# Experts stages of a six-stage transformer kernel: the bias-and-push product on 32-row groups, layer norm sums on ScalarE's accumulator, variance on GpSimd

## The reference

```python
def _L1_ffn_ref(x, router_w, router_b, expert_w, expert_b):
    logits = jnp.einsum('bsd,ed->bse', x, router_w) + router_b
    probs = jax.nn.softmax(logits, axis=-1)
    weights = jnp.max(probs, axis=-1)
    top1 = jnp.argmax(probs, axis=-1)
    y_all = jnp.einsum('bsd,eod->bseo', x, expert_w) + expert_b
    y = jnp.take_along_axis(y_all, top1[:, :, None, None], axis=2)[:, :, 0, :]
    return y * weights[:, :, None]

x = x + 0.5 * _L1_ffn_ref(_layernorm(x), ...)
```

## Time and profile before

| | |
|---|---|
| median of 3 runs | 1595.37 us (1590.17 to 1595.67) |
| profiled execution | 1591.5 us, its span 1589.6 us |
| PE busy | 1541.5 us, 97% of the span |
| DVE busy | 1260.2 us, 79% |
| ACT busy | 936.1 us, 59% |
| POOL busy | 935.5 us, 59% |
| first E stage | about 1184 to 1251 us of the span |
| second E stage | about 1516 to 1588 us, its first batch beside attention |

### The profile page before, as it was taken

How to read it: one execution, slowest core, us unless ns; L and a number is a source line. 1 busy time by engine, 2 the same in 40 slices (tenths; PEclk the granted TensorE clock), 3 DMA queues, 4 the chain that set the end, 5 groups by cost and what they waited for, 6 DMA issues and landing times. The chain is left out here.

```text
span 1589.6 us, 43810 instructions
## 1 busy us (share of the span) xinstructions
PE 1541.5 (97%) x15808; PEld 922.1 (58%) x15808; DVE 1260.2 (79%) x2662; ACT 936.1 (59%) x1826; POOL 935.5 (59%) x806
## 2 busy tenths in 40 slices
PE   7999999999999899799999999999999999999999
PEld 4666666666666666566666666666654434444444
DVE  7976776777877788786777777768778899999877
ACT  6755555555656344365555555556553388888842
POOL 2865756757754399775766756657456334444453
PEclk9999999999999999999999999999999899999999
DMA  4300000000001242100000000000001121112011
GB/s 163 106 8 5 7 0 7 7 0 7 8 1 34 53 84 67 42 6 3 8 1 7 7 0 7 7 0 8 5 12 31 44 61 37 39 39 62 9 42 60
DMA packets 74315, 43.34 MB, mean 27 GB/s; under 512 B 53818, under 2 KB 70842, under 8 KB 74052
## 3 DMA queue, kind: packets, MB, share of 16 engines
q1 hardware_dynamic: 74180, 41.56, 10.9%
HBM read 10.47 MB, written 2.10 MB: 8 GB/s over the span
## 5 line engine op out<-in xcount | busy, mean ns | idle before, releaser
L618 POOL TENSOR_TENSOR scratch<-scratch 128x512 f16<-128x512 f32 x379 | 441.6, 1166 | 375.4 <-ACT scratch L826 375.2
L1395 DVE SCALAR_TENSOR_TENSOR scratch<-psum,scratch 128x512 f32<-128x512 f32 x512 | 352.4, 689 | 235.8 <-PE psum L1979 213.4
L821 ACT ACTIVATE scratch<-psum 128x512 f32<-128x512 f32 x512 | 305.2, 597 | 394.9 <-PE psum L1979 394.0
L2021 PE MATMUL psum<-ffn_down_hi,scratch 128*128 128x128 f16 x2048 | 369.3, 219 | 0.3
L2023 PE MATMUL psum<-ffn_down_hi,scratch 128*128 128x128 f16 x2048 | 369.2, 219 | 0.0
L2022 PE MATMUL psum<-ffn_down_lo,scratch 128*128 128x128 f16 x2048 | 369.2, 219 | 0.0
L826 ACT ACTIVATE scratch<-scratch 128x512 f16<-128x512 f32 x512 | 318.6, 622 | 12.0 <-DVE scratch L1395 11.7
L2021 PEld LDWEIGHTS psum<-ffn_down_hi,scratch 128*128 128x128 f16 x2048 | 200.3, 98 | 59.1 <-POOL scratch L618 0.7
L2022 PEld LDWEIGHTS psum<-ffn_down_lo,scratch 128*128 128x128 f16 x2048 | 200.4, 98 | 58.0
L2023 PEld LDWEIGHTS psum<-ffn_down_hi,scratch 128*128 128x128 f16 x2048 | 200.4, 98 | 0.0
L1977 PE MATMUL psum<-x_hi,ffn_gate_hi 128*128 (+1 forms) x512 | 194.5, 380 | 1.5 <-ACT scratch L821 1.5
(11 more groups left out here) (223 smaller groups left out, 2703.8 us busy)
## 6 DMA issues: line engine op xcount, KB each, us to landing
scratch<-scratch SPq DMA_DIRECT2D x96, 128.0 KB, 2.7
raw<-in_ffn_w_dram SPq DMA_DIRECT2D x8, 768.0 KB, 4.2
ffn_up_hi<-scratch SPq DMA_DIRECT2D x32, 128.0 KB, 2.8
x_tok<-in_x_dram SPq DMA_DIRECT2D x8, 256.0 KB, 7.2
out_dram<-x_tok SPq DMA_DIRECT2D x7, 256.0 KB, 2.2
raw<-in_lin_dram SPq DMA_DIRECT2D x1, 1092.0 KB
x_hi<-scratch SPq DMA_TRANSPOSE x46, 2.3
x_lo<-scratch SPq DMA_TRANSPOSE x46, 2.3
```

The source lines that it names most:

```text
L618: pool.tensor_tensor(h_lo[r], h32[r], h_hi[r], ALU.subtract).then_inc(s_plo, 1)
L821: act.activation(gate_act[k % 2], bank(k % 2), ACT.Silu, scale=W_DOWN).then_inc(s_s, 1)
L1395: dve.scalar_tensor_tensor(h32[k % HSLOTS], bank(5 + k % 2), W_DOWN, gate_act[k % 2], ALU.mult, ALU.mult).then_inc(s_h, 1)
L2021: pe.matmul(dst, h_hi[r][:, cols], hi, start=k % FC == 0 and n == 0, stop=False, skip_group_check=True)
```

## The change

1. **Bias and push on 32-row groups.** The table `e_bias` holds the ten rows (eight push, two bias) four times, at partitions 0, 32, 64 and 96, alternately for the two halves of the experts. `e_not` and `e_out` repeat the mask in each 32-row group. For two tiles at a time, behind the products of both, four matmuls of 32 rows go to four banks. In the last batch, and where the second E stage is woven into attention, it is one tile and two matmuls. The table is filled by 12 small DMAs during the second F stage.
2. **Three pairs of banks.** `expert_banks` gives most tiles one of three pairs instead of two.
3. **Router bias by one matmul.** `logits` issues one 128x32 matmul for the bias of all four tiles instead of four of 128x8.
4. **Statistics on ScalarE.** `prep_sums` (four ACTIVATEs that copy a tile with scale -1/128, the accumulator giving the negative mean `ln_neg`) and `prep_squares` (four that square x plus `ln_neg`, the accumulator giving the sum) replace VectorE's statistics in both E stages, except for batches 2 and 3 of the second. Two of them stand behind each `weigh`. GpSimd's `prep_var` makes the variance of the sums. `prep_sums` waits for the `x_norm` of the batch before, because `ln_neg` is reused.
5. **`x_upper` one tile later.** It now stands ahead of the third `weigh`, before it stood ahead of the second.
6. **No hardware loop** on PE and ACT in the E stages; the bodies are written out.

```diff
+E_GROUP = 32
 # SyncE, between turn_x(3, 0) and turn_x(3, 1)
+            for i in range(4):
+                c = slice(i % 2 * BANK, (i % 2 + 1) * BANK)
+                row = i * E_GROUP
+                sp.dma_start(e_bias[row:row + E, :], bias_w[0:E, c]).then_inc(s_ebias, 16)
+                sp.dma_start(e_bias[row + E:row + E + 1, :], bias_w[32:33, c]).then_inc(s_ebias, 16)
+                sp.dma_start(e_bias[row + E + 1:row + E + 2, :], bias_w[64:65, c]).then_inc(s_ebias, 16)
 # GpSimd
+            def prep_var(n):
+                pool.wait_ge(s_mv, n + SUB)
+                pool.tensor_scalar(ln_var[:], ln_square[:], 1.0 / C, LN_EPS, ALU.mult, ALU.add).then_inc(s_var, SUB)
                     if b + 3 < last:
+                        if not (use and b == 0):
+                            prep_var(n0 + SUB * (b + 3))
                         prep_rstd(n0 + SUB * (b + 3))
                         norm(b + 3)
 # ScalarE
+            def prep_sums(n, s, parts=range(SUB)):
+                if parts[0] == 0:
+                    act.wait_ge(s_xn, n)
+                for q in parts:
+                    ins = act.activation(ln_spent[:, q * P:(q + 1) * P], sub(x_tok, s + q), ACT.Copy, scale=-1.0 / C, accum_out=ln_neg[:, q:q + 1])
+                if parts[-1] == SUB - 1:
+                    ins.then_inc(s_bn, SUB)
+
+            def prep_squares(n, s, parts=range(SUB)):
+                if parts[0] == 0:
+                    act.wait_ge(s_bn, n + SUB)
+                    act.wait_ge(s_var, n)
+                for q in parts:
+                    ins = act.activation(ln_spent[:, q * P:(q + 1) * P], sub(x_tok, s + q), ACT.Square, bias=ln_neg[:, q:q + 1], accum_out=ln_square[:, q:q + 1])
+                if parts[-1] == SUB - 1:
+                    ins.then_inc(s_mv, SUB)
-                        if k == 1 and prep and not (isinstance(b, int) and b == 0):
+                        if k == 2 and prep and not (isinstance(b, int) and b == 0):
                             x_upper(n0 + SUB * b + LEAD)
+                        if stats:
+                            part = range(k % 2 * 2, k % 2 * 2 + 2)
+                            if k < 2:
+                                prep_sums(n0 + SUB * bx, SUB * (bx % NB), part)
+                            else:
+                                prep_squares(n0 + SUB * bx, SUB * (bx % NB), part)
 # VectorE
-                            prep_bn(n0 + SUB * (b + 3), SUB * ((b + 3) % NB))
-                        if k == 2 and b + 3 < last:
-                            statistics(b + 3)
 # TensorE
+                    router_bias = bias_w[:, E * C:E * C + E].rearrange("p (o e) -> p o e", o=1).to_broadcast([P, SUB, E])
+                    pe.matmul(by(bank(7, 0, SUB * E), SUB), ones, router_bias, start=True, stop=True)
-                    pe.wait_ge(s_epick, t + 1)
+                    pe.wait_ge(s_epick, picked_before(t))
+                    for i, k in enumerate(tiles):
+                        for half_of in range(2):
+                            rows = slice((2 * i + half_of) * E_GROUP, (2 * i + half_of + 1) * E_GROUP)
+                            ins = pe.matmul(bank(2 * expert_banks(b * SUB + k) + half_of), e_out[odd][rows, k * P:(k + 1) * P], e_bias[rows, :],
+                                            start=False, stop=True, skip_group_check=True)
+                        ins.then_inc(s_ey, 1)
-                            bias_and_others(b0 + b, k, odd)
+                            if not more:
+                                bias_and_others(b0 + b, (k,), odd)
+                            elif k % 2:
+                                bias_and_others(b0 + b, (k - 1, k), odd)
```

More of the change, by code:

```diff
@@ L650, in body @@
                         if k == 16 and f and next_weights(ph, b):
-                            for t in e_out:
-                                pool.memset(t, 1.0).then_inc(s_erows, 1)
+                            pool.memset(e_not, 1.0 / E_OUT).then_inc(s_erows, 1)
+                            pool.memset(e_bias, 0.0).then_inc(s_erows, 1)
                 body(0, False)
@@ L980, in moe @@
                     begin(act, ph["i"])
-                    others(b0, 0)
+                    others(b0, 0, 4)
                 def body(b, odd, prep, more):
+                    bx = b + 3
+                    stats = bx < (NB + 2 if ph["next"] else NB)
                     for k in range(SUB):
@@ L1660, in moe @@
                     begin(dve, ph["i"])
-                last = NB + 2 if ph["next"] else NB
                 for b in range(use, NB):
@@ L2120, in bias_and_others @@
+                def bias_and_others(b, tiles, odd):
+                    if 0 in tiles:
                         pe.wait_ge(s_eout, b + 1)
-                    for half_of in range(2):
-                        a = half_of * BANK
-                        ins = pe.matmul(bank(2 * (k % 2) + half_of), e_out[odd][:, k * P:(k + 1) * P], bias_w[:, a:a + BANK], start=False, stop=True)
-                    ins.then_inc(s_ey, 1)
-                def others(b, at=4):
+                        if b == 0:
+                            pe.wait_ge(s_ebias, 12 * 16)
+                    for i, k in enumerate(tiles):
[4 more added lines that the diff above has]
+                        ins.then_inc(s_ey, 1)
@@ L2127, in others @@
+                def others(b, at=6):
                     pe.wait_ge(s_enot, b + 1)
                     pe.wait_ge(s_eout, b)
+                    if b == NB + 2:
+                        pe.wait_ge(s_mout, NB)
                     for k in range(SUB):
-                        ins = pe.matmul(bank(at, k * P, (k + 1) * P)[0:E], e_not[:, k * E:(k + 1) * E], ident16, start=True, stop=True)
+                        ins = pe.matmul(bank(at, k * P, (k + 1) * P), e_not[:, k * P:(k + 1) * P], ident16, start=True, stop=True)
```

100 lines of the change are left out of this document (57 added, 43 removed).

## The result

The changed kernel takes 1626.15 us (median of 4 runs, 1624.36 to 1627.92) against 1593.91 (4 runs beside it, 1590.17 to 1595.67): a ratio of 1.020, 95% interval 1.019 to 1.022. It is slower by 32 us. Its profiled execution has a span of 1625.6 us where before had 1589.6, so 36.0 us are to be found between those two.

What follows compares the result with a forecast made beforehand. The late turned x was to bound the experts stages at 10.4 us a batch against 8.17. Terms of +27.2 on 1591.5 gave 1618.7, plus 3.9 of scale 1622.6, plus 3 for the clock: forecast 1625, range 1606 to 1641.

Steps and rivals of the forecast that it cites:

- The ring: Experts stages: first pick, second weigh, sums, x_upper, transfer, logits, product, bias group, next pick; 10.4 us a batch against 8.17.
- the two sums: ScalarE, between the second weigh and x_upper: two sums with accumulator delivery, 0.80 us.
- Accumulator: ScalarE's sums and squares: delivering the accumulator's result costs 0.20 us each, like a small ACTIVATE of its own.
- Bias group: TensorE: four 32-row matmuls, 0.43 us a group; 0.58 us from the products' nominal end until the pick can start.
- first stage, to the third batch: First experts stage up to the third batch's first pick: 14.3 us instead of 9.7, fourth pick 0.5 sooner; +4.1 us.
- its four middle batches: First experts stage, four middle batches at 10.4 us each instead of 8.17; +8.9 us.
- second stage, to the third batch: Second experts stage up to the third batch's first pick: 1546.7 instead of 1540.48; +6.2 us.
- its four batches: Second experts stage: three batches of 10.4 us and one without statistics of 9.6, instead of 32.63; +8.2 us.
- the clock: TensorE's clock falls to 0.50 behind two of eleven waits, up to 1.6 us each; 3 us in all.
- rival 1: TensorE's clock falls in nearly all eleven long batches: +18 us instead of +3, 1640 us; 17 in 100.
- The scale: Whole kernel: the median of the runs lies 3.9 us above the profiled execution, turning 1618.7 into 1622.6.
- a lead of 1.8 us: Before the change, steady batches: the transfer behind x_lower is done at 1208.5, the logits wanting it come at 1210.3.

Runs made afterwards that it cites:

- upper_earlier: The changed kernel with x_upper back behind the first weigh, ahead of the second; 1618.08 us, ratio 1.017.
- logits_behind_pair: The changed kernel with the next batch's logits moved behind the first pair's bias group; 1607.90 us, ratio 1.009.
- bias_singly: The changed kernel with the bias product behind each tile's own products, two 32-row matmuls at a time; 1607.05 us, ratio 1.009.
- before_late_rounding: The kernel before the change, with x_upper behind the second weigh and no longer behind the first; 1609.00 us, ratio 1.010.
- vector_statistics_all: The changed kernel with stats_on_vector's edits, logits behind the first pair, select ahead of the second pick, second stage's batch 1 bias tile by tile; 1593.89 us, ratio 1.000.
- select_first: The changed kernel with x_upper behind the first weigh and the select ahead of the second pick; 1617.31 us, ratio 1.015.
- warm_matmuls: The changed kernel with forty 128x128 products ahead of the wait of logits in batches 2 to 6; 1623.87 us, ratio 1.020.
- stats_on_vector: The changed kernel with the statistics back on VectorE and x_upper ahead of the second weigh; 1602.10 us, ratio 1.006.

## Why the prediction was right, point by point

**The ring.** Predicted 10.4 with an idle of 3.2 us, measured 10.19 with 2.96, in the batches at full clock. Its pieces: rounding done 4.22 us behind the first pick (4.43 in the working), TensorE goes on at 8.03 (8.15), pick 2.16 behind that (2.25). The mis-sized term is the two sums, 0.80 worked out and 0.59 measured; the transfer, 2.48 instead of 2.39, and the way to the pick cancel. Without statistics 9.6 was worked out and 9.60 measured. upper_earlier, logits_behind_pair and bias_singly each change the ring at another place and each shortened the batch.

**Accumulator.** The value taken, 0.20, is about the length of an instruction of its own, as guessed, but its cost in pace is half. Groups by line and shape, ScalarE in the first stage of after:

```profile
L837 ACT ACTIVATE ln_spent<-x_tok 128x128 f16<-128x128 f32 x28 | 8.2, 293 | 2.0 <-POOL x_norm L699 2.0
...
L837 ACT ACTIVATION_READ_ACCUMULATOR ln_spent<-x_tok 128x1 f32 x28 | 5.2, 186 | 0.0
```

**Bias group.** The next form starts 0.33 us behind the group's start, as taken from the earlier trace rows. The pick starts 0.43 behind it (1600.94 to 1601.37), 0.53 behind the nominal end of the products, where 0.58 was taken.

**The terms of the sum**, by first picks in the two profiled executions:

| stretch | predicted | measured |
|---|---|---|
| first stage, to the third batch | +4.1 | 21.84 - 15.74 = +6.1 |
| its four middle batches | +8.9 | 44.73 - 32.67 = +12.1 |
| its end | +0.6 | 16.03 - 14.20 = +1.8 |
| second stage, to the third batch | +6.2 | 29.42 - 21.66 = +7.8 |
| its four batches | +8.2 | 41.57 - 32.63 = +8.9 |
| its end | -0.8 | 11.02 - 12.91 = -1.9 |
| elsewhere | 0 | +1.2 |
| sum | +27.2, and 3 for the clock | +36.0 |

Each stretch but the end of the second stage is longer than worked out although the ring is shorter, and most of this is the clock. It was at 0.50 in seven batches of the two stages, not in two. TensorE rows and windows of after:

```profile
1203.96 0.21 PE L2162 MATMUL psum<-scratch,half_sb 128*128 128x32 f16 x1 [4.50 <-DMA x_lo<-scratch]
1215.89 0.21 PE L2162 MATMUL psum<-scratch,half_sb 128*128 128x32 f16 x1 [3.11 <-DMA x_lo<-scratch]
1227.36 0.19 PE L2162 MATMUL psum<-scratch,half_sb 128*128 128x32 f16 x1 [2.95 <-DMA x_lo<-scratch]
```
```profile
1201.00:1208.00 7.00, 4.04 (x25) 1.39 (x26) 0.37 (x1) 1.85 (x9) 4.63 (x8) 0.56 0.20 40
1216.00:1218.00 2.00, 2.00 (x18) 0.90 (x18) 0.00 (x0) 0.00 (x0) 1.90 (x4) 0.50 0.00 0
...
1596.00:1599.00 3.00, 0.26 (x2) 0.00 (x0) 1.04 (x3) 2.48 (x12) 1.00 (x3) 1.00 0.44 87
1599.00:1602.00 3.00, 2.79 (x27) 1.31 (x28) 0.63 (x1) 0.00 (x0) 2.90 (x6) 1.00 0.26 93
```

The waits of 4.50 and 3.11 were followed by 0.50; those of 2.95 (1227.36) and of 2.96 (1599.21, the last two windows) were not. The length of the wait doesn't decide alone: waits of 2.47 and 2.88 (ended at 1248.97 and 1577.44) were followed by it too, and in before_late_rounding a wait of 0.55 (ended at 1202.62). The Trainium skill (TensorE: Matmul & The Clock Gate, HAM oscillation) describes a kernel whose clock falls each time between bursts parted by waits for DMA; the trace agrees behind six of the eleven waits and not behind the other five. The seventh fall came at the end of the first stage (from 1259.85), behind idle stretches of 1.28 and 1.38; that stretch is 1.2 above the working.

What the falls cost can be read from the batches. Those with a fall among the middle ones lasted 11.71, 11.43, 11.41 and 11.60 in place of 10.19, 1.2 to 1.5 each: the price was right, the count was not. In the batch ahead of the third first pick of each stage, from `logits` to pick took 3.67 (1203.96 to 1207.63) and 3.68 us (1565.72 to 1569.40) in place of 2.16. These six come to 8.4 us where 3 were forecast for all. The shorter ring gave back 1.5. Another 0.5 is a slip of the working: the fourth pick of the first batch was to come 0.5 sooner and didn't, 6.01 us behind the first in both kernels. The 1.2 elsewhere, outside both stages, stays open. It was a middle way between two falls and rival 1.

**The scale.** I added 3.9 us for the way from the profiled execution to the median. The changed kernel's profiled execution took 1627.32 and lies 1.2 above its median. That error of 5 us hides the nearly 6 by which the terms came out too small, the clock above all: the mechanism was right and the ring nearly so, but that the forecast stands within 1.2 us of the result is luck, two errors against each other.

**Where I named the cause too narrowly.** I wrote that a lead of 1.8 us is used up by sums and a later weighing. before_late_rounding shows that the second pick as releaser is enough: it closes a ring with `logits`, and with the falls that came with it this cost 16 us without a single sum and without bias groups. And behind that ring stood others of 8 to 10 us (norm and sums, the meeting of select and GpSimd, rounding in front of squares), which fits that single repairs gave 1 to 18 us.

## What to carry to other kernels

When a step is moved behind another on an in-order engine, write down what its new releaser itself waits for, round to the step again: if the ring closes, its length is the new period, whatever the engines' loads. Taking work off the fullest engine paid nothing here: the bias groups and the later rounding put a producer behind more work, and with both repaired the next engine, VectorE, set the batch at 8.33 us (vector_statistics_all, level with before). After such an edit look first for an engine that idles ahead of one wait in every batch, and try moving the waiting instruction back before anything else (here 18 us for one line).

## What the runs showed of the hardware that I had not expected

- `accum_out` brings a second instruction on ScalarE, ACTIVATION_READ_ACCUMULATOR, 186 ns long, which costs 0.10 us of pace behind a 128x128 activation (two in a row take 0.59 us with it and 0.40 without).
- VectorE operations of two SBUF operands that started during a GpSimd operation over two tensors ended only with it: 0.18 and 0.29 us became up to 1.30 and 1.22. Where VectorE's started first, by as little as 0.02 us, GpSimd's took 1.28 instead of 1.15. Picks from PSUM beside the same GpSimd operations kept their 1.22.
- Four 32-row matmuls of 512 columns on four row groups and four banks took 0.31 to 0.33 us until the next product started, 0.39 with latency, and started 0.31 behind the last product before them (0.22 between products).
- Idle stretches of TensorE near 3 us between 5 to 7 us of matmuls were followed by half clock in some batches and not in others of one execution, and in before_late_rounding one of 0.55 us was. With forty small products ahead of the same wait the clock stayed at 1.00 in the batches they stood in.
- The turning transfer of `x_lo` needed 2.46 to 2.56 us from its row on SyncE to TensorE's start in most batches of the changed kernel and of the runs on it, but 3.11, 3.29, 3.40, 3.97 and 4.10 in single batches of upper_earlier (two), select_first, warm_matmuls and stats_on_vector. These batches were longer by the difference, the last by a fall as well. What delays it stays open.
